# Gated FFN: the last five tiles' transposes ahead of the down products; last FFN: four-tile norm groups, earlier normalising and casting on ScalarE, and 32 products of ones on TensorE

## What is computed

```python
x = x + tanh(g_xattn[0]) * L0_xattn(layernorm(x), ctx, ctx, ...)     # attention 0
x = x + tanh(g_ffn[0]) * L0_ffn(layernorm(x), w_gate, w_up, w_down)  # gated FFN ("FFN 0")
x = x + tanh(g_xattn[1]) * L1_xattn(layernorm(x), ctx, ctx, ...)     # attention 1
x = x + tanh(g_ffn[1]) * L1_ffn(layernorm(x), w1, b1, w2, b2)        # last FFN ("FFN 1")

def L0_ffn(x, w_gate, w_up, w_down):       # ternary weights
    gate = silu(bitlinear(x, w_gate))      # activations rounded to 8 bits per token
    return bitlinear(gate * bitlinear(x, w_up), w_down)

def quant_per_tensor(x):                   # FFN 1: one scale for the whole tensor
    scale = max(max(abs(x)), 1e-6) / 127
    return round(x / scale), scale
```

## Time and profile before

| | us |
|---|---|
| median of 3 runs | 1488.85 |
| lowest and highest | 1488.5, 1491.98 |
| the profiled execution's own time | 1485.42 |
| its span | 1483.6 |
| attention 0, up to some 800 | the longest stage |
| end of FFN 0 (tile 63's add) | 1049.4 |
| end of attention 1 (last next_max) | 1298.6 |
| first gelu of FFN 1 | 1305.5 |

### The profile page before, as it was taken

One profiled execution on the slowest core, in us unless ns is written; L12 is line 12 of the kernel. 1 busy time (PEld: TensorE's weight loads), 2 busy tenths in 40 slices (PEclk: granted clock), 3 DMA queues, 4 the chain that ended last, 5 costly groups with the idle time before them and its releaser, 6 DMA issues.

```text
span 1483.6 us, 30813 instructions
## 1 busy us (share of the span) xinstructions
PE 1327.3 (89%) x11555; PEld 898.3 (61%) x11610; DVE 1170.1 (79%) x1896; ACT 1062.9 (72%) x1795; POOL 762.5 (51%) x1215
## 2 busy tenths in 40 slices
PE   4799999999999999999987999998789889287696
PEld 3466666666666666666644666666667666243384
DVE  3477887887888888877778999986547999888896
ACT  2377777777777777777757888887455665689996
POOL 2156766756766666765773443331204676667000
PEclk9799999999999999999969999999999998599899
DMA  9666867856766866855420000000455453068199
GB/s 150 110 117 109 136 112 122 149 95 133 128 114 121 128 125 102 137 100 97 88 66 1 1 1 1 1 1 1 128 161 132 102 150 97 0 257 339 39 405 379
DMA packets 125605, 172.01 MB, mean 116 GB/s; under 512 B 47490, under 2 KB 78338, under 8 KB 120066
## 3 DMA queue, kind: packets, MB, share of 16 engines
q1 hardware_dynamic: 124688, 169.24, 49.4%
q10 hardware_dynamic: 768, 0.79, 0.5%
HBM read 79.22 MB, written 38.80 MB: 80 GB/s over the span
## 4 chain that ended last, share of the span: by engine, by line
PE 62%; DVE 12%; ACT 12%; DMA 5%; issue 4%; POOL 3%; SPq 2%; ACTq 0%; DVEq 0%; POOLq 0%
PE psum L574 10%; PE psum L585 9%; PE psum L561 7%; PE psum L602 5%; PE psum L549 4%; ACT f_gelu L1997 4%; PE psum L619 4%; PE psum L976 3%; PE psum L1002 3%; PE psum L994 3%; ACT f_gelu L2006 3%; PE psum L523 2%; DMA f_gelu<-g_scratch 2%; PE psum L536 2%; DVE f_hid L1104 2%
## 5 line engine op out<-in xcount | busy, mean ns | idle before, releaser
L764 DVE TENSOR_REDUCE neg_max<-psum 128x8 f32<-128x1024 f32 x256 | 313.2, 1224 | 70.4 <-PE psum L561 65.7
L695 ACT ACTIVATE exp_t<-psum 128x512 f32<-128x512 f32 x512 | 281.6, 598 | 50.5 <-PE psum L574 50.4
L869 POOL TENSOR_TENSOR rs<-rs,minus_half 128x16 f32<-128x16 f32 x64 | 186.3, 2911 | 5.0
L574 PEld LDWEIGHTS psum<-q_stack,k_stack 50*128 50x128 f32 x2048 | 135.0, 188 | 77.6 <-issue 73.3
L574 PE MATMUL psum<-q_stack,k_stack 50*128 50x128 f32 x2048 | 171.1, 287 | 0.8 <-ACT exp_t L695 0.8
L585 PE MATMUL psum<-exp_t,v_pad 128*32 128x256 f32 x2048 | 166.7, 398 | 0.0
L561 PE MATMUL psum<-k_stack,q_stack 48*128 48x256 f32 x1024 | 134.1, 340 | 15.0 <-DVE neg_max L764 11.7
L700 ACT ACTIVATE o_t<-psum 128x512 f32<-128x512 f32 x128 | 76.5, 598 | 92.4 <-PE psum L585 92.3
L861 POOL TENSOR_TENSOR sq<-u 128x256 f32<-128x256 f32 x64 | 39.2, 612 | 175.9 <-DVE u L781 175.1
L976 PE MATMUL psum<-f_w,f_xqt 128*128 128x512 bf16 x481 | 117.7, 385 | 7.2 <-DVE f_hid L1104 4.5
L561 PEld LDWEIGHTS psum<-k_stack,q_stack 48*128 48x128 f32 x1024 | 81.0, 189 | 67.2 <-issue 48.2
(11 more groups left out here) (224 smaller groups left out, 3035.3 us busy)
## 6 DMA issues: line engine op xcount, KB each, us to landing
k_stack<-k_hi SPq DMA_DIRECT2D x252, 128.0 KB, 4.7
g_scratch<-f_gelu SPq DMA_DIRECT2D x21, 1024.0 KB, 4.5
f_gelu<-g_scratch SPq DMA_DIRECT2D x21, 1024.0 KB, 15.1
k_stack<-k_lo SPq DMA_DIRECT2D x126, 128.0 KB, 5.0
ctx_t<-in_ctx_t SPq DMA_DIRECT2D x32, 256.0 KB, 5.4
x_state<-in_x SPq DMA_DIRECT2D x16, 512.0 KB, 6.8
v_in<-in_ctx SPq DMA_DIRECT2D x32, 256.0 KB, 5.6
v_scratch<-v_in SPq DMA_DIRECT2D x32, 256.0 KB, 5.5
```

What stands on the lines that cost most here:

```text
L574: r = e.matmul(psum[:, 2 + j, o:o + P], self.k_st[rows, b // 2 % self.NK, pair // 2 % 2, pair % 2, i, pair // 4, b % 2, :], self.q_st[rows ...
L695: e.activation(self.prob[:, n % 3, j].rearrange("p n w t -> p (n w t)"), psum[:, 2 + j, :], ACT.Exp).then_inc(s["exp"], 1)
L764: e.tensor_reduce(self.negm[:, b % 2, :, :, 2 * u:2 * u + 2].rearrange("p j w n -> p j n w"), psum[:, 0:2, :].rearrange("p j (n w k) -> p ...
L869: e.tensor_tensor(self.rs[:, i], self.rs[:, i], self.expo[:, :], ALU.pow).then_inc(s["pool"], 1)
```

## The change

Five edits. (1) In FFN 0's steps from 64 on, PE does `turn_h(b - 6)` before `down(b - 7)`. (2) Tiles 59, 61 and 63 are turned through PSUM banks 2 and 3, which the up products no longer need once all `f_hid` are made, and 60 and 62 through 4 and 5, so that `turn_h(b)` waits only for `h_turned(b - 2)`. (3) The norm group of tiles 48 to 55 becomes two groups of four. (4) On ACT, `act_normalise(0)` moves to step 32, `act_cast(0)` and `act_normalise(1)` are in step 33, `act_normalise(2)` and `(3)` in step 34, and `act_cast(1)` goes behind the last `next_normed`. (5) PE gets 32 products of ones, bf16, 512 columns each, into bank 7, whose result nobody reads: four each time `next_max` has passed 24, 25, ... 31 pairs.

```diff
-    GROUPS = [...] + [[(8 * g, 8) for g in range(7)] + [(56, 4), (60, 4)]]
+    GROUPS = [...] + [[(8 * g, 8) for g in range(6)] + [(b, 4) for b in range(48, 64, 4)]]
...
+    LATE = NSEQ - 5
+    def turned_bank(self, b):
+        return 2 if b >= self.LATE and (b - self.LATE) % 2 == 0 else 4
...
         def turn_h(b):
+            bank = self.turned_bank(b)
             w.wait_ge(a0.s["x_new"], NSEQ)
             w.wait_ge(s["hr"], b + 1)
-            w.wait_ge(s["ht_sb"], b)
+            if b < self.LATE:
+                w.wait_ge(s["ht_sb"], b)
+            else:
+                w.wait_ge(s["hid"], NSEQ)
+                w.wait_ge(s["ht_sb"], b - 1)
...
+            if b >= NSEQ and b - 6 < NSEQ:
+                turn_h(b - 6)
             if 0 <= b - 7 < NSEQ:
                 down(b - 7)
             if 0 <= b + 2 < NSEQ:
                 turn_x(b + 2)
-            if 0 <= b - 6 < NSEQ:
+            if b < NSEQ and 0 <= b - 6:
                 turn_h(b - 6)
...
+        w.wait_ge(self.fw.s["dve"], self.fw.INV)
+        w.wait_ge(s["g_sb"], 16)
+        w.wait_ge(s["qt_sb"], self.NP)
+        w.wait_ge(s["cols"], 2)
+        dense = sh.ones[:, :].bitcast(BF16)
+        for n in range(24, self.NP):
+            w.wait_ge(s["next_max"], n)
+            for _ in range(4):
+                e.matmul(psum[:, 7, :], dense[:, 0:P], dense.unsqueeze(1).to_broadcast([P, 2, 2 * P]), start=True, stop=True)
...
-            if i in (self.NP + 1, self.NP + 2):
+            if i == self.NP:
 
                 w.wait_ge(s["s_pe"], self.NP)
-                self.fw.act_cast(w, i - self.NP - 1)
-            if self.NP + 3 <= i < self.NP + 7:
-                self.fw.act_normalise(w, i - self.NP - 3, self.minus)
+                self.fw.act_normalise(w, 0, self.minus)
+            if i == self.NP + 1:
+                self.fw.act_cast(w, 0)
+                self.fw.act_normalise(w, 1, self.minus)
+            if i == self.NP + 2:
+                self.fw.act_normalise(w, 2, self.minus)
+                self.fw.act_normalise(w, 3, self.minus)
+            if i == self.NP + 11:
+                self.fw.act_cast(w, 1)
```

More of the change, by code:

```diff
@@ L77, in sems @@
         return {n: self.sem(prefix + n) for n in names}
-    GROUPS = [[(0, 2), (2, 6)] + [(8 * g, 8) for g in range(1, 8)]] + [[(8 * g, 8) for g in range(8)]] * 2 + [[(8 * g, 8) for g in range(7)] + [(56, 4), (60, 4)]]
+    GROUPS = [[(0, 2), (2, 6)] + [(8 * g, 8) for g in range(1, 8)]] + [[(8 * g, 8) for g in range(8)]] * 2 + [[(8 * g, 8) for g in range(6)] + [(b, 4) for b in range(48, 64, 4)]]
     def group(self, k, b):
@@ L989, in turn_h @@
         def turn_h(b):
+            bank = self.turned_bank(b)
             w.wait_ge(a0.s["x_new"], NSEQ)
             w.wait_ge(s["hr"], b + 1)
-            w.wait_ge(s["ht_sb"], b)
+            if b < self.LATE:
[3 more added lines that the diff above has]
+                w.wait_ge(s["ht_sb"], b - 1)
             for i in range(self.NHT):
-                r = e.transpose(psum[:, 4 + i // 4, i % 4 * P:(i % 4 + 1) * P], self.hr[:, b % 2, i * P:(i + 1) * P], sh.ident[:, :])
+                r = e.transpose(psum[:, bank + i // 4, i % 4 * P:(i % 4 + 1) * P], self.hr[:, b % 2, i * P:(i + 1) * P], sh.ident[:, :])
             r.then_inc(s["ht_pe"], 1)
@@ L1053, in h_turned @@
             w.wait_ge(s["down_pe"], b - 1)
-            e.activation(self.hqt[:, b % 2].rearrange("p n t -> p (n t)"), psum[:, 4:6, :].rearrange("p j c -> p (j c)"), ACT.Copy,
+            bank = self.turned_bank(b)
+            e.activation(self.hqt[:, b % 2].rearrange("p n t -> p (n t)"), psum[:, bank:bank + 2, :].rearrange("p j c -> p (j c)"), ACT.Copy,
                          bias=-ROUND).then_inc(s["ht_sb"], 1)
```

## The result

The changed kernel takes 1471.11 us (median of 4 runs, 1470.03 to 1472.35) against 1488.67 of the kernel before (4 runs, 1480.27 to 1491.98): the ratio is 0.9902, 95% interval 0.9875 to 0.993. The forecast was 1474.5 with a range of 1469 to 1481. In a later session the same pair gave 1474.54 against 1484.17, ratio 0.9935 (0.9913 to 0.9957), 9.6 us less in place of 17.6.

The account below looks back on a forecast made before the run. It took a PE-bound bulk as unchanged, with gains at two seams: latency in FFN 0's tail and ACT's pace ending attention 1. 10.6 + 3.0 + 0.7 = 14.3 us off 1488.85 gave 1474.5, range 1469 to 1481.

Parts of the forecast that it names:

- The bound: A PE-bound bulk left alone; gains only at FFN 0's tail (latency) and the end of attention 1 (ACT sets the pace).
- The tail: FFN 0's tail, edits 1 and 2: period 1.96 us instead of 3.03, tile 63's add at 1038.33, 10.6 us less.
- The clock in the tail: FFN 0's tail: clock holds at 1.00, 10.6 us less; rival: it falls to 1.2 GHz, 7.6 less, chance 0.15.
- The norm edits: End of attention 1, edits 3 and 4: last next_normed ends at 1294.90 instead of 1297.91, 3.0 us less.
- POOL's new group: End of attention 1: a group of four takes 3.0 us, fitting the 4.48 us POOL waited before a_fac.
- The cover behind the second cast and the table load: ACT before FFN 1: both done by about 1298.2, first work due near 1299.6, 1.4 us of cover.
- The ones: Before FFN 1, edit 5: products of ones raise PE's clock early; between +1.1 and -0.9, taken as 0.7 us less.
- The gain at the far side: Path to the first gelu at full clock: 0.84 us on eight transposes plus some 0.3 elsewhere, 1.1 us.
- the cost in the queue: PE's queue before the spread of the maximum: products of ones end 0.4 us late, or 2.0 at slower prices.
- The rivals: Tail clock falls 1477.5 (0.15); ones fail 1483.4 (0.12); POOL delays 1475.5-1477.5 (0.07); no tail overlap 1482.2 (0.04); slower 1493+ (0.03).
- the lottery the other way: Attention 1's loop over pairs: one half-clock stretch fewer than before, giving 1469.7 us; chance 0.07.
- The price of a stretch: Attention 1's loop, 1230 to 1240: 10 us with PE busy at half clock loses 4.8 us.

Follow-up runs that it names:

- norm-only kernel: The kernel before with only edits 3 and 4; 1485.82 us against 1484.34, ratio 0.9998.
- split kernel: The changed kernel with the last five down products in banks 6 and 7 in turn and FFN 1's weights loaded in four pieces; 1468.46 us, ratio 0.9898.
- old-groups: The changed kernel without edit 3, tiles 48 to 55 in one norm group of eight; 1465.4 us, one run.

## Why the prediction was right, point by point

**The bound.** Both seams were read rightly: the tail was latency between PE and ACT, and the second seam was ACT's queue. All three gains add up to the end of the kernel, since the rest is unchanged at 178 us.

**The total, 14.3 forecast.** That the measured 1471.11 lies so near 1474.5 is in part luck. The sum was taken off 1488.85, the median of three runs; later sets of the same kernel have medians of 1484.34 (15 runs) and 1484.17 (11). Less 14.3, that would have been 1470, where the changed kernel took 1474.54. The first session shows 17.6 us less and the second 9.6; the seams are 13.9 in the profiles, and the differences lie outside them or in the old kernel's own clock, which the second session has no profile of.

**The tail, 10.6 forecast, 9.7 measured.** The method, old times run through the new order link by link, gave the period (1.96; 1.94 measured) and the start. The term mis-sized is its last one: `h_turned(63)` 1.06 after that of 62 (1.30 measured), and `down(63)` 1.08 behind it (1.50). It left out that `down(63)` waits for tile 62's add (`x_new`), which the code says plainly; the chain shows `down(62)` at 1032.85, its add at 1033.76, `down(63)` at 1034.39. With two banks for `down` that wait went, and 0.4 of the 0.9 came back. The other 0.5 is that `f_hqt` of tile 58 starts 0.3 later than by the links I took, and that of 63 falls another 0.2 behind.

**The clock in the tail.** It held at 1.00, as chosen between the bounds, in all eleven profiles with the new order on PE. That 2.4 us of the gain belong to a half-clock stretch of before was said; what wasn't is that this stretch is not always there: the norm-only kernel had the old order without it.

**The norm edits, 3.0 forecast, 3.02 measured.** DVE's `next_max` paces pairs 24 to 27, then it is 0.98 us a pair, as forecast. POOL's new group fits in front of `a_fac`, but with luck: priced at 3.0 us after the cheapest of the old groups, it took 4.4 (1261.66 to 1266.05) and ended 0.15 before `a_fac` started. But the text gave the credit to both edits, and edit 3 earned none of it. The working already showed it: pair 24's early start is swallowed by the wait of pair 26 for DVE. The cover behind the second cast and the table load is 0.64 us in the changed kernel, where 1.4 were forecast.

**The ones, 0.7 forecast, 1.2 measured.** The gain at the far side was sized well (1.1 forecast), the cost in the queue was not there: no 0.4 us late, 0.0 and 0.09 in the two profiles. In the first the clock rose with 4.2 us of products done, where I had 5.2 (scaled down from 5.8 before, which the trace puts nearer 5.7). What the sum missed is larger: the term was priced against the kernel before, where the clock rose in time for the first hidden products. In both profiles with the norm edits and without the ones it rose after them. So by the traces this edit is worth about 4 us (1.8 + 2.2) in the company of the others, and without it the norm edits keep 1.1 of their 3.0 us in the one profile and 0.4 in the other. The terms are right as a sum of edits and not each alone; that the kernel before had its clock in time, so that the sum came out, was not seen. Nor do the ones always keep what they win: in the split kernel the entry and the rest are together 2.4 us longer than in the first profile of the changed kernel.

**The rivals.** None came true as a whole; the measured median is 3.4 us below the forecast, near the 1469.7 of the lottery the other way, and the profile doesn't show one stretch fewer in attention 1. The price of a stretch, 4.8 us for 10 us at half clock, is not borne out as a rule: between the changed kernel and old-groups the middle differs by 5.6 us with 17 us more at half clock (30.7 against 13.7, without the stretch in which PE falls idle at the end), 3.3 for 10.

## What to carry to other kernels

In a tail where two engines hand one buffer back and forth, put the next tile's first half in front of this tile's second half and give it its own PSUM banks: here 3.03 us a tile became 2.27 by the order and 1.94 by the banks. Price an edit in the company of the others: of 3 us taken off an idle stretch in front of a matmul stage, 1.9 went into a longer time at TensorE's lower clock, until dummy products brought the clock up first. A gain of 3 us per edit can't be seen in totals that scatter by 10; cutting the traces at fixed instructions shows it to 0.1 where the clock is the same in both, and not where it differs (the old tail took 21.23 or 23.7).

## What the runs showed of the hardware

- Float32 transposes alone lift TensorE's clock from 1.2 to 2.4 GHz: 64 of them in 9.14 us, the rise at 1280, PE idle for 15.5 us before them.
- The rise didn't move with the start of PE's work: without ones it came 27.3 to 27.5 us after the last `a_fac` in four profiles, 5.6 us after PE took up work in two and 8.6 in the other two.
- A stretch that the edits leave alone differs from run to run: the middle was 225.2 to 238.1 us over the thirteen profiles without the split load, with 17.7 to 57.4 us of it at half clock. The seams of the changed kernel agreed to 0.1 us in its two profiles.
- Once up, the clock need not stay up: in the split kernel it was full at the spread of the maximum and fell at about 1283.7, ahead of the first hidden products, with all 32 products of ones in front, and the entry took 7.29 us. PE there:

```profile
1281.93 1.09 PE L1967 MATMUL psum<-ident,f_xn 128*128 128x128 f32 x8 [1.04 <-DVE f_xn L2064]
1283.45 0.84 PE L1967 MATMUL psum<-ident,f_xn 128*128 128x128 f32 x4 [0.42 <-DVE f_xn L2064]
1284.52 2.97 PE L1979 MATMUL psum<-f_xqt,f_w_up 128*128 128x512 bf16 x7 [0.23 <-issue]
```
